# Loading expert 1's weights piece by piece, and at two other places of a DMA queue, in a fused attention and mixture-of-experts kernel

## The reference

```python
# 1: a learned adjacency of the context, the top 153 of each row kept, made symmetric
Q, K = h @ Wq.T, h @ Wk.T
sim = (Q K^T summed over 4 heads) / (sqrt(32) * 4)
A = sigmoid(sim) * (sim >= 153rd largest of the row)
x = x + (1 - gamma) * layernorm(x) + gamma * (A + A.T) / 2
# 2: a mixture of 16 experts, each token goes to 4 of them
t = layernorm(x)
score = softmax over the top 4 of (t @ router.T + bias)
gate, up = (t @ gate_up[e] + bias)[even], [odd]      # 512 -> 1024
y_e = ((clip(up) + 1) * min(gate, 7) * sigmoid(1.702 * gate)) @ down[e] + bias
x = x + sum over the token's 4 experts of score * y_e
```

## Time and profile before

| what | us |
|---|---|
| median of 3 runs | 918.02 (916.44 to 924.27) |
| the profiled execution | 915.97 |
| its span, first to last instruction | 914.1 |
| PE busy | 775.8 (85%) |
| DVE, ACT, POOL busy | 597.1, 402.7, 311.2 |
| first stage and change-over, until tile 4 starts on PE | 256.0 |

### The profile page before, as it was taken

One profiled execution on the slowest core, in us unless ns is written; L12 is line 12 of the kernel. 1 busy time (PEld: TensorE's weight loads), 2 busy tenths in 40 slices (PEclk: granted clock), 3 DMA queues, 4 the chain that ended last, 5 costly groups with the idle time before them and its releaser, 6 DMA issues.

```text
span 914.1 us, 16473 instructions
## 1 busy us (share of the span) xinstructions
PE 775.8 (85%) x3568; PEld 625.6 (68%) x3569; DVE 597.1 (65%) x1087; ACT 402.7 (44%) x663; POOL 311.2 (34%) x353
## 2 busy tenths in 40 slices
PE   4464826179779999999999999999999999989893
PEld 1134425167668878878888887878788878868682
DVE  4678759586755486776666857776776576675442
ACT  3998758622322254345252433543452345242221
POOL 1331626576422323233232333323333222222221
PEclk9665555559989999999999999999999999999998
DMA  8501111326526463865636547467656365622332
GB/s 279 193 0 47 46 38 56 47 71 197 129 44 183 95 179 77 225 171 129 182 91 180 160 113 217 111 164 216 178 139 170 60 183 117 175 49 46 58 48 40
DMA packets 70706, 112.10 MB, mean 123 GB/s; under 512 B 29888, under 2 KB 32192, under 8 KB 70592
## 3 DMA queue, kind: packets, MB, share of 16 engines
q1 hardware_dynamic: 33024, 74.22, 24.2%
q0 software_dynamic: 18416, 36.53, 20.8%
q10 hardware_dynamic: 19152, 0.14, 1.1%
HBM read 84.05 MB, written 28.90 MB: 124 GB/s over the span
## 4 chain that ended last, share of the span: by engine, by line
PE 65%; ACT 9%; issue 7%; DVE 7%; DMA 4%; SPq 2%; ACTq 2%; POOL 1%; DVEq 1%; another core or an unknown queue 0%; POOLq 0%
PE gate_up_ps L879 36%; PE bank L879 21%; PE bank L861 3%; PE bank L869 3%; ACT marks L542 3%; ACT bgu L542 1%; DMA bd_raw<-_ffn_down_proj_bias_dram 1%; DMA out_dram<-x_sb 1%; ACT xn L573 1%; ACT x_sb L555 1%; DMA raw_w<-in_L_ffn_down_proj_dram 1%; ACT w L681 1%; DMA out_dram<-yb,aslot 1%; PE gate_up_ps L768 1%; DVE hl L1080 1%
## 5 line engine op out<-in xcount | busy, mean ns | idle before, releaser
L879 PE MATMUL gate_up_ps<-w,xh 128*128 (+1 forms) x1152 | 366.2, 399 | 7.3 <-DVE w L1105 5.6
L879 PEld LDWEIGHTS gate_up_ps<-w,xh 128*128 128x128 f32 x1152 | 213.2, 190 | 50.0 <-DVE w L1105 6.1
L454 POOL DMA_INDIRECT out_dram<-yb,aslot x72 | 130.5, 1812 | 295.8 <-ACT yb L662 214.1
L879 PE MATMUL gate_up_ps<-w,xl 128*128 (+1 forms) x576 | 227.0, 394 | 0.1
L879 PE MATMUL bank<-w,hh 128*128 (+1 forms) x576 | 182.0, 397 | 15.7 <-DVE hl L1080 15.0
L655 ACT ACTIVATE sg<-gc 128x512 f32<-128x512 f32 x72 | 45.6, 634 | 222.7 <-DVE gc L1090 210.2
L879 PEld LDWEIGHTS bank<-w,hh 128*128 128x128 f32 x576 | 108.3, 190 | 45.3 <-issue 23.2
L445 POOL DMA_INDIRECT xg<-xn_rows,gslot x75 | 76.8, 1023 | 180.2 <-DMA gslot<-slot_rows 160.9
L1080 DVE TENSOR_TENSOR hl<-bank,hh 128x512 fp32r<-128x512 f32 x72 | 49.6, 689 | 135.5 <-ACT hh L649 130.8
L1086 DVE TENSOR_TENSOR gu<-gate_up_ps,bgu 128x1024 f32<-128x1024 f32 x72 | 88.1, 1224 | 69.2 <-PE gate_up_ps L879 48.5
L879 PEld LDWEIGHTS gate_up_ps<-w,xl 128*128 128x128 f32 x576 | 109.3, 190 | 23.9
(11 more groups left out here) (221 smaller groups left out, 799.1 us busy)
## 6 DMA issues: line engine op xcount, KB each, us to landing
raw_w<-_L_ffn_gate_up_proj_dram SPq DMA_DIRECT2D x64, 512.0 KB
raw_w<-in_L_ffn_down_proj_dram SPq DMA_DIRECT2D x64, 256.0 KB
bgu<-n_gate_up_proj_bias_dram SPq DMA_DIRECT2D x16, 512.0 KB
x_sb<-in_x_dram SPq DMA_DIRECT2D x4, 1024.0 KB, 11.2
xn_rows<-xn SPq DMA_DIRECT2D x4, 1024.0 KB
out_dram<-x_sb SPq DMA_DIRECT2D x4, 1024.0 KB
xg<-xn_rows,gslot POOLq DMA_INDIRECT x75
out_dram<-yb,aslot POOLq DMA_INDIRECT x72
```

Of the source, the lines that this page charges most:

```text
L454: pool.indirect_dma_start(out_v, bass.IndirectOffsetOnAxis(aslot[:, k, 0:1], 0), yb[:, k % 2, :], None, bounds_check=TOKENS - 1, oob_is_er ...
L879: last = nc.tensor.matmul(out_ps, lhs[:, rows], w[:, bass.ds(buf, 1), part, c, cols].rearrange("p a d -> p (a d)"), start=(m == 0), stop=( ...
```

## The change

Only SP's program changes. Expert 1's first half is issued ahead of the slots of tiles 2 and 3 and of batch 3's normalised rows; its second half behind batch 3's base rows and the slots of tiles 4 to 7. Within both halves of expert 1, each piece is issued only when the one before has landed (`done` is counted by 16 a piece). The other experts are loaded as before.

```diff
                     sp.dma_start(raw_w[:, c, 0:GU], gate_up[:, c, :]).then_inc(done, 16)
+                    if isinstance(e, int) and e == 1:
+                        sp.wait_ge(done, at + 16)
                     sp.dma_start(raw_w[:, c, GU:WIDE], down[:, c, :]).then_inc(done, 16)
                     at += 32
                     if c == 0:
+                        if isinstance(e, int) and e == 1:
+                            sp.wait_ge(done, at)
                         sp.dma_start(bgu[:, bias_at, :], bias.broadcast_to([P, GU])).then_inc(done, 16)
...
                 if b == EARLY:
+                    sp.wait_ge(gathered[0], 16)
+                    sp.wait_ge(S["lo_done"], HALF)
+                    load_half(1, 0, 1)
                     sp.wait_ge(scat[EARLY - 1], 16 * RT * TOP_K)
                     for k in range(2, UNROLL):
...
-                if b == EARLY:
-                    sp.wait_ge(gathered[0], 16)
-                    for h in range(2):
-                        sp.wait_ge(S["lo_done"], HALF * (h + 1))
-                        load_half(1, h, 1)
-                        for T in range(UNROLL + 2 * h, UNROLL + 2 * h + 2):
-                            sp.wait_ge(gathered[T % UNROLL], 16)
-                            sp.dma_start(gslot[:, T % UNROLL, :], slot_d[first_block(T) * P:(first_block(T) + 1) * P, :]
-                                         ).then_inc(gslot_in[T % UNROLL], 16)
                 sp.wait_ge(S["bo_done"], RT * (b + 1))
                 sp.dma_start(out_v[rows, :].rearrange("(r p) h -> p r h", p=P), x_sb[:, b * RT:(b + 1) * RT, :]).then_inc(S["acc_out"], 16)
 
+            for T in range(UNROLL, FROZEN):
+                k, first = T % UNROLL, first_block(T) * P
+                sp.wait_ge(gathered[k], 16)
+                sp.dma_start(gslot[:, k, :], slot_d[first:first + P, :]).then_inc(gslot_in[k], 16)
+            sp.wait_ge(S["lo_done"], HC)
+            load_half(1, 1, 1)
             sp.wait_ge(S["words_done"], 1)
```

## The result

The changed kernel takes 926.71 us (median of 14 runs, 921.93 to 930.44) against 921.6 (14 runs, 916.44 to 927.02) of the kernel before on the same chip: ratio 1.0071, 95% interval [1.0047, 1.0094], or 4.3 to 8.7 us more. It is outside the predicted range. The kernel before is itself 3.6 us above the median of three runs that the forecast started from; the ratio leaves that out. The profiled execution has a span of 926.7 us, against 914.1 before. About half of that difference is chance: the profiled execution of before (915.97 us) was faster than all fourteen of its timed ones.

A forecast was written before the change was run, and what follows sets the result against it. PE's chain of products was taken as the bound, so a shift of tile 4's start goes into the end. 915.97 + 1.6 = 917.6 us for the profiled execution, 2.05 more for the median: 919.6, range 914 to 925.

The forecast's parts named there:

- S: Time when gather 2's rows arrive and PE can transpose tile 2's rows: 221.6 us, bounds 216.5 to 227.5.
- The 4.24 us gap: PE's idle time before tile 1's transpose at 232.50, put down to DVE's late addition; forecast to go.
- 0.59 of wait for DVE at 222.53: PE's wait between tile 2's transpose and tile 1's down product; deducted if DVE is not held up.
- 1.63 of slow products: Two PE products before 240.94 taking 7.09 us instead of 5.46; deducted, then 1.6 us of slow work added behind S.
- the hold-up: Late start of DVE's addition for tile 1 beside output rows and first piece: 1.0 us put, bounds 0 and 5.9.
- its long gap: DVE's 5.87 us idle before its addition for tile 1; its return would show the prediction wrong.
- rival 2: DVE's or ACT's hold-up returns whole, or pieces are as slow as their upper bound: 922.4 to 924.5 us; 20%.
- Gather 4: POOL's gather behind batch 3's scatters: issued at 239.5, there at 243, costed at nothing.
- rival 3: Expert 1's second half lands after 252.7 and becomes the bound, slower by over 1%: 928 to 930 with rival 2; 4%.
- Rivals 1 and 4: 1: gather 2 shares with batch 3's write, 917.6 us, 25%. 4: gain of 4 us or more, 911.9 us, 5%.
- rival 1: Gather 2 moves beside batch 3's write instead of behind it: S = 219.6, time 917.6, or 915 with short pieces; 25%.
- The line of 3.0 and 4.0 us: SP's piece times: 3.0 us for 256 KB, 4.0 for 512 KB; four waits sum to 15.0, bounds 12.0 and 17.8.

The follow-up runs named there:

- e7: The changed kernel with the slots of tiles 2 and 3 ahead of expert 1's first half: 0.9981 of the kernel before.
- e1: The changed kernel without its waits between pieces, both halves kept at their new places: 1.0004 of the kernel before.
- e6: The kernel before with only the waits between expert 1's pieces added: 1.0034 of the kernel before.
- e14: The changed kernel with slots of tiles 2 and 3 ahead of the first half and batch 3's scatters split 8 and 8: 0.9926 of the kernel before.
- e5: The kernel before with batch 3's 16 scatters left out: 0.9861 of the kernel before.
- e3: The changed kernel with the second half's four pieces cut to 16 columns each: 1.0065 of the kernel before.
- e8: The changed kernel with the write of batch 3's base rows cut from 512 to 16 columns: 1.0045 of the kernel before.
- e9: The changed kernel with batch 3's base rows and expert 1's second half both cut to 16 columns: 1.0054 of the kernel before.
- e2: The changed kernel with batch 3's 16 scatters left out: 0.9937 of the kernel before.

## Why the prediction was wrong

- **SP's part was right.** Down piece at 213.50 (213.1 said), slots at 213.88 (213.5), gather 2 at 217.13 (216.5), S = 221.86 (221.6), PE idle 5.66 us (5.5), lower clock behind it (1.6 us for the products, as said), output rows at 226.02 (226.5). Some of that is luck: the pieces began 0.9 us earlier than forecast and their four waits took 1.3 us longer in all. e7, and e1 beside it (1.0004), show that this chain, from the slots behind the pieces, is the loss; e6 and e14 leave room for some 0.3% of the waits' own.
- **The 4.24 us gap went, as said**: 234.95 has none. The step that failed comes next: "4.24 idle, 0.59 of wait for DVE at 222.53 and 1.63 of slow products go", with 1.0 put back for the hold-up, "bounds 0 and 5.9". DVE had its long gap again, 11.96 us before 247.20, which the prediction had named as a sign that it is wrong, and tile 4 began at 267.87 (257.6). In the profiled execution it came back as 0.46 + 1.70 + 6.74 = 8.90 us of idle PE, and slow products behind that. In the medians it costs the same in both kernels, 1.39% and 1.34%, within the uncertainty given with e5. So nothing may be deducted: 1.6 + 4.24 + 0.59 + 1.63 - 1.0 = 7.1 us, and 6.5 (4.3 to 8.7) were measured, where the forecast had 1.6. That 7.1 lies so near 6.5 is partly luck, since the interval is 4.4 us wide. This is rival 2, which had 20%.
- **Why it was mis-sized.** I had seen that the gaps stood beside bulk transfers (0.79 of DMA time), and took them to go with these. e3, e8 and e9 take the bulk away and keep the gaps; e2 and e5 take the scatters away and lose them. The row that spoke was in the earlier trace rows: sixteen scatters from 211.87 to 232.26, with all three gaps inside that time or just behind it. The change moved this row by 7.8 us, so the hold-up moved with it.
- **Gather 4** was forecast for 239.5 (240.09) and costs nothing, as said. **The second half** (rival 3) was issued until 248.68, later than forecast: its pieces held SP for 5.9, 7.3 and 5.7 us, where 4.0, 3.0 and 4.0 were put, so that it landed after 248.68 and not by 246. ACT's split followed directly on its scaling at 262.31, so it stayed hidden behind the delay in front of it. In e6 the same slowness showed.
- **Rivals 1 and 4** did not happen: the gather came behind the 1 MB write, as the forecast had it. In the trace's packets the write ends and the gather begins between 219.5 and 220.0. By the Trainium skill's rule that each DMA engine takes turns between queues ("DMA: Bandwidth & Descriptors", Queues, rings and completion order) it would have come at 219.6, by rival 1's estimate; the trace has 221.86. The rule speaks of queues that have work, and whether the gather's packets were ready before 219.5 the trace doesn't tell.
- **The start was off.** The median of three runs was 3.6 us below that of fourteen, and the profiled execution of before lower still. With a spread of 10 us between executions, 3.6 of the 7.1 us between the forecast (919.6) and the median have that source; from 918.02 the ratio gives 924.5, just inside the range. The mechanism was wrong all the same: 6.5 us more than before were measured and 1.6 forecast.

## What to carry to other kernels

When a wait is cut short by a change, ask whether its cause goes or only its place: a gap whose releaser the program doesn't explain must not be deducted until something removes it. Small requests on which a chain hangs (slot rows for a gather) belong ahead of large pieces with waits between them, not behind. In this kernel a row of 16 indirect scatters was best broken into groups of 4 to 8 with other work of the queue between them, but not by waiting for them ahead of a gather that somebody needs.

## What the runs showed of the hardware

With 16 indirect scatters of 128 rows issued in a row, one per 1.27 us, PE's signals reach ACT and DVE late, by up to 11 us in the changed kernel and 14 in e1 (transposition over at 231.30, ACT at 245.25). It begins some 7 to 13 us after the first scatter, wherever they stand (212 to 232, 220 to 240 or 251 to 272 us), and needs no large transfer beside it (e9, DMA engines busy for 0.11 to 0.21 of their time). PE itself goes on at its higher clock (1.00 from 230 to 240 us in the changed kernel and in e9), but in several of the traces with stops in the middle of a product: 0.46 and 1.70 us in the changed kernel, 0.49, 1.70, 1.03, 1.50 and 0.81 in e3. The kernels without the scatters are faster by about 13 us of 920, those with the row broken up by about 10. Groups of 8 leave single gaps of 3 to 4 us; groups of 4 leave none, nor do 16 with a wait for landing after every fourth. How scatters hold up a signal between two other engines was not found: the trace shows when the signals come, not what they wait for.

A piece of 512 KB alone on SP's queue took 4.8 us the first time and 3.75 for the bias of equal size; 256 KB took 4.6 and 512 KB then 3.2. The line of 3.0 and 4.0 us through the rows of before was near in the sum of four (16.3 against 15.0, inside its bounds), and off by 0.25 to 1.6 us for each. The Trainium skill's fit ("DMA: Bandwidth & Descriptors", Anatomy of one DMA) gives, by an estimate from it, 3.2 and 2.6 us; one of the four reached it. The page has it for DMAs that POOL issues, and these were SP's.
